# Latent attention: one step for a pair of heads, scores in two row tiles, causal mask added by TensorE

## The chip, the cores and the metric

The kernel runs on one core of a Trainium2 chip. The metric is device time in microseconds (us), from the start to the end of one execution; lower is better. Engines are named as in the profile: PE is TensorE's matmul, PEld its weight load, DVE is VectorE, ACT is ScalarE, POOL is GpSimd, SP is the queue that issues most DMAs. PSUM is the accumulator memory of PE: 8 banks of 512 float32 in each of 128 partitions.

## What is computed

A sandwich of two transformer layers on x of 1024 x 256. Each of the four parts is `x = x + layernorm(part(layernorm(x)))`: a 16-head attention without mask over one sequence of 1024, a ternary feed-forward part, a latent attention, and a feed-forward part whose weights are looked up in a table of 16 values. The change is in the third part, the latent attention, reduced here to what matters (1024 positions, 16 heads, latent width 64):

```python
c_kv = x @ Wdkv.T                                  # 1024 x 64, shared by all heads
q_lat = einsum('bhtd,hdl->bhtl', q, k_eff)         # a 64-wide query for each head
scores = einsum('bhtl,bsl->bhts', q_lat, c_kv) / sqrt(16)
scores = where(causal, scores, finfo.min)          # 16 heads x 1024 x 1024, lower triangle
attn = softmax(scores)                             # float32
ctx = einsum('bhts,bsl->bhtl', attn, c_kv)
y = einsum('bhtl,hld->bhtd', ctx, v_eff)           # 16 wide for each head
```

## The kernel before

Everything stays on the chip between the parts. Each engine has its own list of steps in program order (`order_of_latent` for this part), and semaphores tie the lists together. A step such as `("row_max", h, i8, part)` is read by all engines: each issues what is its own.

Heads are taken in pairs p (heads 2p and 2p+1) and in four groups g of two pairs. For a pair, these steps follow one another:

- `project` (line 1238 on PE): query and key rows of the pair into one PSUM bank. ACT writes a first part (line 1515, for keys also line 1520), then DVE (line 1802, queries) or POOL (line 2021, keys; line 1811 on DVE for the pair 0) subtracts. The keys of the two heads stand in different halves of the 128 partitions of `KT[p % 4]`, with zeros in the other half (`keys_zero` on POOL), so that one product over 128 partitions with a query that holds both heads gives one head's scores.
- `row_max` (line 1250 on PE, line 1829 on DVE): for each head and each block i8 of 128 queries the scores against the keys up to the diagonal, in one or two parts of at most 512 columns. DVE adds the mask, writes the sum back into PSUM and takes the row maximum in one custom instruction, which a short register read follows.
- `shift` (line 1260 on PE, line 1839 on DVE): the maxima of half of the positions are transposed by PE and subtracted from the queries by DVE, so that the exponent later needs no bias.
- `weights` (line 1271 on PE, line 1529 on ACT, line 2028 on POOL): scores again, transposed (keys on partitions), for one head and one block k of 128 keys; ACT takes the exponential into the buffer `ET`, POOL clears what lies above the diagonal in the first 128 columns. In the last group they are called `weights3` (lines 1296, 1539 and 2035) and are taken by halves of the positions.
- `combine` (line 1285 on PE; `combine3`, line 1310): four heads of a group at once, each in a column tile of 32 of PE's 128 columns, accumulated into banks 6 and 7.
- `heads_out` (line 1320): the result is transposed and divided by its sum.

PSUM banks 0 to 5 are a ring. Every product except `combine` takes the next bank in program order, and PE may write it once the engine that read that bank six takes earlier has released it:

```python
def take_ring(step, release):
    i = take(step, "ring", 6)
    BANK[step] = (i, free_ring[i])
    free_ring[i] = release
```

What stands next to what is set by `merge`, which interleaves two lists of steps in proportion to written costs: `behind(g)` holds the weights, shifts and combines of group g, `ahead(g)` the maxima and projections of the next pairs. In each group five combines (k from 0 to 4) stand among many weights; then the maxima of the group's next pair stand almost alone, with four projections between them; then come the three last combines, and the next group's weights start.

## Time and profile before

| | before |
|---|---|
| runs | 936.48 us median of 3 (935.08 to 939.54) |
| profiled execution, own time | 935.9 us |
| its span in the profile | 934.2 us |
| mean granted PE clock | 0.98 of full speed |
| latent attention, scores and combines | about 676 to 872 us of the span |

The span is what the trace covers; about 1.7 us of the profiled execution lie around it. The stage of the change is about a fifth of the span. "Idle before" is the time for which an engine stood still ahead of an instruction, with what ended it; a matmul's end is modelled, so the distance between two starts tells more than a matmul's duration.

### The profile page before, as it was taken

The numbers are of one execution on the slowest core, as the hardware profiler recorded it, in microseconds if no ns is written. First come the engines' busy times: TensorE is split into PE (matmuls) and PEld (weight loads), VectorE is DVE, ScalarE is ACT, GpSimd is POOL, SyncE is SP. The second block draws the span as 40 slices with busy tenths as digits, with TensorE's granted clock in tenths as the row PEclk, the third lists the DMA queues.
The fourth block names the chain that finished last, engine by engine and source line by source line (L and its number), as shares of the span: only waits on it lengthen the run. The fifth ranks groups of instructions, "written<-read, shape, count | busy, mean of one in ns | idle before, by whom it ended". The sixth has DMA issues, their size and how long they took to land.

```text
span 934.2 us, 12935 instructions
## 1 busy us (share of the span) xinstructions
PE 845.1 (90%) x4314; PEld 584.5 (63%) x4314; DVE 763.8 (82%) x1567; ACT 590.6 (63%) x990; POOL 413.8 (44%) x425
## 2 busy tenths in 40 slices
PE   4799989999999999999999998688877999998996
PEld 2566666676577577667667665457654555554686
DVE  3588999899998999999999998575599787876635
ACT  3476866776777666667667667364555767657533
POOL 2124444444344357778777771161323434433301
PEclk9999999999999999999999999789989999999999
DMA  3379757868777678668768767130000000000001
GB/s 110 65 154 170 138 111 167 175 129 149 167 154 147 128 136 158 136 128 158 155 109 147 130 133 144 35 105 1 1 1 0 1 1 1 2 1 1 1 1 45
DMA packets 276851, 86.29 MB, mean 92 GB/s; under 512 B 267568, under 2 KB 272432, under 8 KB 276400
## 3 DMA queue, kind: packets, MB, share of 16 engines
q1 hardware_dynamic: 275504, 80.05, 44.0%
q0 software_dynamic: 992, 5.34, 2.0%
q8 instruction: 34, 0.56, 0.3%
q14 instruction: 33, 0.27, 0.1%
q10 hardware_dynamic: 288, 0.07, 0.1%
HBM read 17.29 MB, written 1.05 MB: 20 GB/s over the span
## 4 chain that ended last, share of the span: by engine, by line
PE 51%; DVE 28%; issue 8%; ACT 7%; DMA 4%; POOL 1%; SPq 0%; ACTq 0%; POOLq 0%; DVEq 0%
PE ps L1033 11%; PE ps L1034 10%; PE ps L1035 10%; DVE nmax L1644 6%; DVE EP L1659 5%; PE ps L1056 4%; DVE ps L1829 3%; PE ps L1070 3%; PE ps L1285 3%; PE ps L1271 3%; DMA ET<-EP 2%; DVE ptm L1743 2%; PE ps L1250 2%; ACT EP L1435 1%; DVE st L1574 1%
## 5 line engine op out<-in xcount | busy, mean ns | idle before, releaser
L1435 ACT ACTIVATE EP<-ps,rinv 128x1024 f16<-128x1024 f32 x128 | 142.7, 1115 | 52.8 <-DVE rinv L1654 51.6
L1659 DVE SCALAR_TENSOR_TENSOR EP<-ps,rinv,EP 128x1024 f16<-128x1024 f32 x128 | 163.7, 1279 | 11.1 <-ACT EP L1435 10.4
L1425 ACT ACTIVATE ps<-ps,nmax 128x1024 f32<-128x1024 f32 x128 | 139.5, 1090 | 36.7 <-DVE nmax L1644 36.0
L1644 DVE TENSOR_REDUCE nmax<-ps 128x1 f32<-128x1024 f32 x128 | 154.9, 1210 | 1.4 <-PE ps L1035 1.2
L1966 POOL TENSOR_TENSOR wgu<-wgu,ptm 128x688 f32<-128x688 f32 x60 | 100.7, 1679 | 42.8 <-DVE ptm L1743 40.2
L1033 PE MATMUL ps<-ET,VH 128*128 128x512 f16 x256 | 98.8, 386 | 21.0 <-DMA ET<-EP 15.1
L1033 PE MATMUL ps<-KH,QH 128*128 128x512 f32 x256 | 106.6, 416 | 8.4 <-DVE KL L1626 4.7
L1966 POOL TENSOR_TENSOR wdn<-wdn,ptm 128x512 f32<-128x512 f32 x45 | 58.6, 1303 | 95.4 <-DVE ptm L1743 93.9
L1035 PE MATMUL ps<-KH,QL 128*128 128x512 f32 x256 | 100.6, 393 | 0.0
L1034 PE MATMUL ps<-KL,QH 128*128 128x512 f32 x256 | 100.3, 392 | 0.0
L1034 PE MATMUL ps<-ET,VH 128*128 128x512 f16 x256 | 98.2, 384 | 0.0
L1035 PE MATMUL ps<-ET,VL 128*128 128x512 f16 x256 | 98.0, 383 | 0.0
L1529 ACT ACTIVATE ET<-ps 128x512 f32<-128x512 f32 (+3 forms) x144 | 62.5, 498 | 36.9 <-PE ps L1271 36.2
L1829 DVE CUSTOM_DVE_ANT_0 ps<-ps,tern 128x512 f32<-128x512 f32 (+3 forms) x128 | 71.7, 603 | 15.0 <-PE ps L1250 14.9
L1893 POOL TENSOR_TENSOR rs<-ve,mhalf 128x4 f32<-128x4 f32 (+1 forms) x21 | 19.4, 922 | 123.1 <-DVE ve L1579 98.4
L1033 PEld LDWEIGHTS ps<-ET,VH 128*128 128x128 f16 x256 | 25.2, 98 | 61.0 <-DMA ET<-EP 21.1
L1033 PEld LDWEIGHTS ps<-KH,QH 128*128 128x128 f32 x256 | 48.2, 188 | 23.8 <-issue 6.8
L2028 POOL TENSOR_SCALAR_AFFINE_SELECT ET<-ET 128x128 f32<-128x128 f32 x96 | 28.2, 294 | 64.1 <-ACT ET L1529 57.3
L1033 PE MATMUL ps<-XH,wqh 128*128 128x512 f32 x128 | 55.0, 430 | 1.5 <-DVE VL L1636 1.0
L1035 PEld LDWEIGHTS ps<-KH,QL 128*128 128x128 f32 x256 | 48.0, 188 | 11.0
L1034 PEld LDWEIGHTS ps<-KL,QH 128*128 128x128 f32 x256 | 48.3, 189 | 7.8
L1034 PE MATMUL ps<-XL,wqh 128*128 128x512 f32 x128 | 51.7, 404 | 0.0
(237 smaller groups left out, 2166.7 us busy)
## 6 DMA issues: line engine op xcount, KB each, us to landing
wqr<-in_wqk SPq DMA_DIRECT2D x16, 256.0 KB, 3.8
wgu<-in_tern POOLq DMA_DIRECT2D x3, 1024.0 KB, 6.4
wvr<-in_wv SPq DMA_DIRECT2D x8, 256.0 KB, 4.3
wor<-in_wo SPq DMA_DIRECT2D x16, 128.0 KB, 3.1
ET<-EP SPq DMA_TRANSPOSE x128, 4.4
X<-in_x SPq DMA_DIRECT2D x2, 512.0 KB, 6.1
prw<-in_down_idx POOLq DMA_DIRECT2D x2, 256.0 KB, 6.2
tern<-in_l_wuq_rep SPq DMA_DIRECT2D x1, 512.0 KB, 4.6
```

The source lines that it names most:

```text
L1033: e.matmul(dst, lh, rh, start=first, stop=False)
L1034: e.matmul(dst, lh, rl, start=False, stop=False)
L1035: return e.matmul(dst, ll, rh, start=False, stop=last)
L1056: mm = e.matmul(ps[:, 2 * r + o, :], l, m, start=i == 0, stop=i == len(pairs) - 1)
L1425: e.activation(bank, bank, ACT.Exp, bias=nmax[:, c:c + 1], scale=1.0, accum_out=rsum[:, c:c + 1]).then_inc(exped.sem, 1)
L1435: e.mul(EP[:, n % NE_RING, 0, :], SB(u, j), rinv[:, c:c + 1]).then_inc(e_hi.sem, 1)
L1529: e.activation(ET[:, r, c:c + n1], ps[:, BANK[(*step, c)][0], n - n1:n], ACT.Exp).then_inc(weight_exped.sem, 1)
L1644: e.tensor_reduce(nmax[:, c:c + 1], SB(u, j), AX.X, ALU.max, negate=True).then_inc(maxed.sem, 1)
L1659: e.scalar_tensor_tensor(out=EP[:, n % NE_RING, 1, :], in0=SB(u, j), scalar=rinv[:, c:c + 1], in1=EP[:, n % NE_RING, 0, :], op0=ALU.mult, ...
L1829: e.tensor_tensor_reduce(src, src, mask[:, m0:m0 + n], 1.0, -3.0e38 if part == 0 else half, ALU.add, ALU.max, NM[:, p % 2, i8, col:col + 1 ...
L1966: e.tensor_tensor(dst, dst, ptm[:, v % 2, 0:n], ALU.add).then_inc(lut_added.sem, 1)
L2028: e.affine_select(out=tile, in_=tile, compare_op=ALU.is_ge, fill=0.0, base=0, pattern=[[1, P]], channel_multiplier=-1).then_inc(masked.sem, 1)
```

## The change

Scores, maxima, exponentials and selections are now steps of a pair, not of a head.

1. Keys: each pair has its own 128 x 1024 tile, one head in partitions 0 to 63 and the other in 64 to 127. The zero halves, and the POOL memsets that wrote them, are gone. A pair's key subtraction is one instruction over 128 partitions, not two over 64.
2. Scores: for each step PE issues two products of 64 rows each, one in each row tile (`tile_position` (0, 0) and (64, 0)), into two neighbouring banks.
3. Mask: for the part that holds the diagonal, PE adds the mask with two more products (a 128 x 128 identity by a 128 x 128 mask, both bfloat16, over the full 128 rows).
4. Maxima: DVE takes them with one ordinary reduction over both banks; for blocks of two parts a short `join_max` takes the larger. Nothing is written back into PSUM.
5. Exponentials and selections: one ACT instruction and one POOL instruction for both heads.
6. The ring: scores of a pair take two banks, starting at an even one, so six banks are three pairs. A product that needs one bank and stands between two pairs leaves the bank beside it unused.

```diff
 def maxima(p):
-    return [(0.1 + 0.001 * cuts(P * (i8 + 1))[part][1], ("row_max", 2 * p + hh, i8, part))
-            for i8 in range(8) for part in range(1 + i8 // 4) for hh in range(2)]
+    return [(0.1 + 0.002 * cuts(P * (i8 + 1))[part][1], ("row_max", p, i8, part))
+            for i8 in range(8) for part in range(1 + i8 // 4)] + [(0.05, ("join_max", p))]
...
-    KT = [QH, QL, KH, KL]
+    KT = [t[:, i, :] for t in (KL, QH, QL, KH) for i in range(2)]
+    halves = [slice(0, 64), slice(64, 128)]
...
+    def take_ring_pair(step, release):
+        count["ring"] += count["ring"] % 2
+        i = take(step, "ring", 6)
+        count["ring"] += 1
+        BANK[step] = (i, free_ring[i:i + 2])
+        free_ring[i] = free_ring[i + 1] = release
...
@@ PE, row_max @@
-    e.matmul(ps[:, i, 0:n], QT(p)[:, i8 * P:i8 * P + P], KT[p % 4][:, hh, c:c + n],
-             start=True, stop=True).then_inc(max_scored.sem, 1)
+    for hh, rows in enumerate(halves):
+        mm = e.matmul(ps[:, i + hh, 0:n], QT(p)[rows, i8 * P:i8 * P + P], KT[p][rows, c:c + n],
+                      start=True, stop=part < i8 // 4, tile_position=(64 * hh, 0))
+    if part == i8 // 4:
+        w.wait_ge(*mask_set["ident"])
+        for hh in range(2):
+            mm = e.matmul(ps[:, i + hh, P * i8 - c:P * i8 - c + P], ident_b, mask_b,
+                          start=False, stop=True)
+    mm.then_inc(max_scored.sem, 1)
...
@@ PE, weights (weights3 alike) @@
-    e.matmul(ps[:, i, 0:n], KT[p % 4][:, h % 2, k * P:k * P + P], Q2[p % 4][:, q0:q0 + n],
-             start=True, stop=True).then_inc(weighed.sem, 1)
+    for hh, rows in enumerate(halves):
+        mm = e.matmul(ps[:, i + hh, 0:n], KT[p][rows, k * P:k * P + P], Q2[p % 4][rows, q0:q0 + n],
+                      start=True, stop=True, tile_position=(64 * hh, 0))
+    mm.then_inc(weighed.sem, 1)
...
@@ DVE, row_max @@
-    e.tensor_tensor_reduce(src, src, mask[:, m0:m0 + n], 1.0, -3.0e38 if part == 0 else half,
-                           ALU.add, ALU.max,
-                           NM[:, p % 2, i8, col:col + 1] if last else half).then_inc(row_maxed.sem, 1)
+    e.tensor_reduce(NMC[p % 2][:, i8, :] if i8 < 4 else m1[:, p % 2, i8 - 4, part, :],
+                    ps[:, i:i + 2, 0:n], AX.X, ALU.max).then_inc(row_maxed.sem, 1)
...
@@ ACT, weights @@
-    e.activation(ET[:, r, c:c + n1], ps[:, BANK[(*step, c)][0], n - n1:n],
-                 ACT.Exp).then_inc(weight_exped.sem, 1)
+    e.activation(ET[:, 2 * r:2 * r + 2, c:c + n1], ps[:, i:i + 2, n - n1:n],
+                 ACT.Exp).then_inc(weight_exped.sem, 1)
```

Where one group ends and the next begins, PE's program holds these rows before (the opening of group 2: the two short combines, line 1285, then weights of line 1271, maxima of line 1250, shifts of line 1260; the number behind x counts equal rows in a run):

```order
L1285 MATMUL ps<-ET,VX 32x256 x4
L1285 MATMUL ps<-ET,VX 32x128 x4
L1271 MATMUL ps<-XL,QH 128x512 x2
L1250 MATMUL ps<-KH,XH 128x256 x4
L1271 MATMUL ps<-XL,QH 128x512 x2
L1250 MATMUL ps<-KH,XH 128x384 x2
L1250 MATMUL ps<-KH,XH 128x512
L1271 MATMUL ps<-XL,QH 128x512
L1271 MATMUL ps<-XL,QH 128x384
L1250 MATMUL ps<-KH,XH 128x512
L1250 MATMUL ps<-KH,XH 128x384
L1260 MATMUL ps<-ident,NM 128x128 x4
```

At the same place PE's program holds these rows after (line 1284 weights, line 1256 maxima, line 1261 masks, line 1273 shifts, line 1299 combines; each x2 of lines 1284 and 1256 is one pair, one product in each row tile):

```order
L1299 MATMUL ps<-ET,VX 32x256 x4
L1299 MATMUL ps<-ET,VX 32x128 x4
L1284 MATMUL ps<-XL,QL 128x512 x4
L1256 MATMUL ps<-KH,XH 128x256 x2
L1261 MATMUL ps<-tern 128x128 x2
L1256 MATMUL ps<-KH,XH 128x256 x2
L1261 MATMUL ps<-tern 128x128 x2
L1256 MATMUL ps<-KH,XH 128x384 x2
L1261 MATMUL ps<-tern 128x128 x2
L1256 MATMUL ps<-KH,XH 128x512 x2
L1261 MATMUL ps<-tern 128x128 x2
L1273 MATMUL ps<-ident,NM 128x128 x4
```

Both heads' weights now stand together (two pairs of 512 columns in a row), then four pairs of maxima, each with its masks, where weights and maxima of single heads took turns; the first shift stands behind the fourth pair of maxima.

DVE's program at the same place before: a custom instruction for each head, a register read behind each, one shift (line 1839) between them.

```order
L1829 ISA ps,NM<-ps,tern 128x384
L1829 ISA NM 128x1
L1829 ISA ps,NM<-ps,tern 128x512
L1829 ISA NM 128x1
L1829 ISA ps,NM<-ps,tern 128x512
L1829 ISA NM 128x1
L1839 TENSOR_TENSOR Q<-XH,ps 128x512
L1829 ISA ps,M<-ps,tern 128x384
```

And after: line 1846 is the join of the pair before, line 1839 now the reductions, line 1854 the shifts, line 1819 and line 1862 a projection's subtraction and a `heads_out`.

```order
L1846 TENSOR_TENSOR NM<-M 128x8
L1839 TENSOR_REDUCE NM<-ps 128x2 x4
L1854 TENSOR_TENSOR XL<-XH,ps 128x512
L1839 TENSOR_REDUCE M<-ps 128x2
L1854 TENSOR_TENSOR XL<-XH,ps 128x512
L1839 TENSOR_REDUCE M<-ps 128x2 x2
L1819 SCALAR_TENSOR_TENSOR XH<-ps,pat,R 128x512
```

A reduction of both heads stands where two custom instructions and two reads stood; the order of maxima, shifts and projections is kept.

## Rows read from the trace of the kernel before

**Rows 1.** Busy time by stretch: us, each engine's busy (instructions), granted clock, DMA.

```profile
676.00:727.00 51.00, 40.99 (x157) 26.51 (x155) 46.00 (x149) 29.43 (x55) 14.44 (x21) 0.91 0.00 1
...
727.00:747.00 20.00, 19.35 (x134) 10.82 (x134) 13.16 (x44) 13.90 (x31) 10.11 (x21) 1.00 0.01 1
747.00:773.00 26.00, 23.71 (x108) 13.97 (x106) 22.24 (x76) 17.07 (x35) 11.25 (x19) 1.00 0.01 1
...
839.00:872.00 33.00, 29.38 (x178) 13.72 (x172) 19.35 (x58) 25.03 (x61) 14.37 (x42) 1.00 0.01 2
```

**Rows 2.** Chain that ended last, by line: 676 to 727, then 727 to 840 us.

```profile
by line: DVE ps L1829 37.1%; issue 18.4%; ACT R L1515 6.9%; DVE NM L1829 5.7%; PE ps L1271 4.3%; DVE XL L1839 3.5%; DVE Q L1802 3.0%; DVE M L1829 2.8%; ACT tern L1520 2.8%; DVE QH L1811 2.7%; ACT ET L1529 2.3%; DVE XL L1591 2.1%; DVE XH L18
...
by line: PE ps L1285 24.4%; PE ps L1271 21.1%; PE ps L1250 16.0%; DVE ps L1829 9.9%; issue 7.9%; ACT ET L1529 4.2%; ACT R L1515 3.5%; PE ps L1238 3.0%; PE ps L1260 2.9%; PE ps L1320 1.7%; DVE XH L1802 1.3%; DVE NM L1829 1.3%; ACT tern L1520
```

**Rows 3.** Pieces of that chain, 773 to 798 us: start, us, what.

```profile
773.23 1.85 PE ps L1285 x16
...
777.75 1.64 PE ps L1285 x16
...
780.06 0.23 PE ps L1271
780.29 0.23 PE ps L1250
...
782.46 1.43 PE ps L1285 x16
...
789.12 0.99 PE ps L1285 x8
...
797.47 0.78 PE ps L1285 x8
```

**Rows 4.** DVE maxima and a plain reduction, groups: busy, mean ns | idle.

```profile
L1644 DVE TENSOR_REDUCE nmax<-ps 128x1 f32<-128x1024 f32 x128 | 154.9, 1210 | 1.4 <-PE ps L1035 1.2
...
L1829 DVE CUSTOM_DVE_ANT_0 ps<-ps,tern 128x512 f32<-128x512 f32 x64 | 44.5, 720 | 6.1 <-PE ps L1250 6.0
L1829 DVE CUSTOM_DVE_ANT_0 ps<-ps,tern 128x128 f32<-128x128 f32 x16 | 4.6, 313 | 6.1 <-PE ps L1250 6.1
```

**Rows 5.** DVE busy of line 1829 alone: opening stretch, and all stretches.

```profile
676.00:727.00 51.00, 32.54 (x123) 0.91 0.00 1
...
sum 163.00, DVE 106.09; mean DVE 17.68
```

**Rows 6.** Exponentials on ACT, groups.

```profile
L1425 ACT ACTIVATE ps<-ps,nmax 128x1024 f32<-128x1024 f32 x128 | 139.5, 1090 | 36.7 <-DVE nmax L1644 36.0
...
L1529 ACT ACTIVATE ET<-ps 128x512 f32<-128x512 f32 x60 | 34.2, 605 | 17.5 <-PE ps L1271 17.2
```

**Rows 7.** Timeline: a product whose bank was late, and its reader.

```profile
753.36 0.39 PE L1271 MATMUL ps<-XL,QL 128*128 128x256 f32 x1 [0.16 <-DVE M L1829]
...
753.84 0.38 ACT L1529 ACTIVATE ET<-ps 128x256 f32<-128x256 f32 x1 [0.43 <-PE ps L1271]
```

**Rows 8.** Timeline of PE, opening of group 2.

```profile
801.06 0.73 PE L1271 MATMUL ps<-XL,QH 128*128 128x512 f32 x2
...
805.75 0.60 PE L1260 MATMUL ps<-ident,NM 128*128 128x128 f32 x4
806.10 0.91 PE L1250 MATMUL ps<-KH,XH 128*128 128x256 f32 x2
807.05 0.98 PE L1271 MATMUL ps<-XL,QH 128*128 128x512 f32 x2
807.99 0.74 PE L1238 MATMUL ps<-CS,QW 128*128 128x512 f32 x2
...
817.44 1.06 PE L1285 MATMUL ps<-ET,VX 128*32 128x512 f32 x8
```

**Rows 9.** A weight load of the scores, and the key split of pair 0.

```profile
L1250 PEld LDWEIGHTS ps<-KL,XH 128*128 128x128 f32 x48 | 8.9, 188 | 3.4 <-DVE XH L1802 1.2 <-DVE NM L1829 0.7 <-DVE M L1829 0.5
...
L1811 DVE TENSOR_TENSOR QH<-tern,R 64x512 fp32r<-64x512 f32 x4 | 2.7, 687 | 1.9 <-ACT tern L1520 1.8
```

## Prediction before the run

> **What bounds the kernel now.** I first read the busy time by stretch [rows 1], because the stage of the change (about 676 to 872 us) has no single bound. From 676 to 727 us DVE is busy for 46.0 of 51 us: the maxima of the first two pairs. From 727 to 747 us, where combines stand among weights, PE is busy for 19.4 of 20 us; two more such stretches follow (773 to 791 and 817 to 839), 60 us in all. Between them lie stretches like 747 to 773 us: PE 23.7, DVE 22.2 and ACT 17.1 of 26 us, so nothing is free and nothing is full. In the last group (839 to 872 us) ACT is busy for 25.0 of 33 us.
>
> The chain says the same [rows 2]. In the opening stretch DVE's maxima (line 1829) hold 37% of it. From 727 to 840 us PE holds it: the combines 24.4%, the scores of lines 1271 and 1250 together 37.1%, which is 42 us; DVE's maxima hold 9.9%. The pieces [rows 3] show how it runs there: score after score at 0.23 us for 512 columns, then a combine, with no wait between them.
>
> So PE work removed would show in 60 us, DVE work in some 100 us. That is the most the change can move; what it can lose is in the ring of banks.
>
> **PE.** Before, 336 score products with a mean of 453 columns (counted in the program): at 0.23 us for 512 columns [rows 3], 68 us. If the two row tiles run together, half goes: -34 us of PE time. The trace has no row tile. Its nearest rows are the combines in four column tiles [rows 3]: 1.85, 1.64 and 1.43 us for 1024, 896 and 768 columns, so 0.21 us for every 128 columns, all four heads and both passes of float32 together. Their single instructions, laid end to end, would need several times that, so tiles do run at once in this kernel. 1024 columns at that rate are 1.70 us, and 0.15 us is left for entering and leaving the tiles. New are 64 steps with two mask products. A 128-column product lies between 0.06 us (a quarter of 0.23) and 0.09 us (four transposes in 0.35 us, [rows 8]), and each mask step also leaves the row tiles and comes back, 0.15 us: about 0.3 us a step, 19 us. In program order the mode changes rise from 64 to 227; apart from the 128 around masks that is 35 more, 3 us at half of 0.15. PE's balance is -12 us if row tiles overlap, and +22 us if not.
>
> [...]
>
> **DVE.** Line 1829 is busy for 106.1 us over eight pairs [rows 5], 13.3 us a pair, each of its 192 instructions with a register read. Its forms give 1.06 ns a column (720 against 313 ns over 384 columns, [rows 4]). The plain reduction of line 1644 takes 1210 ns for 1024 columns [rows 4], so 125 ns beside its columns. A pair needs 12 reductions over 9216 columns: 9.8 + 1.5 = 11.3 us, and a join, at most 0.2 us. That saves 1.9 us a pair; if reductions can't overlap at their ends as the custom ones do, about 1.2 us. Over the stage it is 9 to 15 us. Pair 0's key split, four instructions of 0.69 us [rows 9], becomes two: -1.4 us.
>
> **ACT and POOL.** A pair of 512 columns costs 1.09 us at most (line 1425, [rows 6]) against twice 0.605 us; back to back the two overlap, so I give ACT nothing. POOL halves its key splits and loses its memsets, but nothing of this lies in the chain [rows 2]; I count 0, and if it showed, at most one 0.7 us piece.
>
> **The ring.** This is where I think the gain goes. Six banks were six tiles; now they are three pairs, and a projection, shift or heads_out between two pairs takes a pair's place. In program order the ring's takes rise from 456 banks to 495, 39 of them unused. A place is held from the first write until its reader is done. From a late bank's product to its reader's start it is 0.48 us [rows 7]; where the weights are there earlier I take 0.42, with masks 0.62, and 0.05 us back to PE. Reading takes 1.06 us (exponentials of 1024 columns), 1.21 us (maxima of 1024).
>
> I placed the rows of the opening of group 2 under these rules, from the end of the last combine. Two exponentials' scores fill places 1 and 2 at 0 and 0.25, the first maxima place 3 at 0.5. The second maxima need place 1: the exponential runs from 0.42 to 1.48, so 1.53. The third need place 2: the second exponential ends at 2.44, so 2.5. The fourth follow at 2.95 and the first shift at 3.4 in the places that DVE has left. The next maxima wait for the third reduction (4.0), so 4.05; the second shift waits for the fourth (5.15), so 5.2. Two more places on, the next weights start at 6.8, the projection of queries at 8.4, and the next group's first combine at 18.3. In the trace [rows 8], counted from 801.06 us, the second shift stands at 4.7, the weights at 6.0, the projection at 6.9 and the combine at 16.4. The same rules with six single places put that combine at 16.5, so they can be trusted to a few tenths. **This opening gets 1.9 us longer**; it occurs twice in full (758 to 773 and 801 to 817 us).
>
> The same placement from 775.08 (end of a combine) to 801.06 us puts the next combines at 2.5, 7.0 and 14.15 us, and the first short one at 23.6; in the trace they stand at 2.7, 7.4, 14.0 and 22.4 us [rows 3]. The end comes at 26.1 against 26.0 us. PE no longer works there all the time, but waits for places as long: **no gain in the combine stretches**.
>
> A late place costs more with two loads: a score's load is 188 ns [rows 9], and the second tile's may follow the first. Between 0 and 0.2 us for each of some 186 places, three at a time, is 0 to 12 us; most waits overlap others, so I take +3, a quarter.
>
> **Sum.** Opening stretch: 32.5 us of maxima [rows 5] are 2.45 pairs, -4.7 at best, -2.9 at 1.2 us a pair, and -1.4 for the key split; part returns as waits for places, so -4 (bounds -6 and 0). Combine and maxima stretches 0. Two openings +3.8. Late places +3. Last group: half its scores come free, but ACT sets the pace, -1. Together +1.8: 935.9 + 1.8 = 937.7 us for the profiled execution, which stands 0.6 us under the median of the runs. I predict **938.3 us**.
>
> **Rivals.**
> - *Places turn over in time.* If a pair's fill hides behind the other two, the engines' own savings count: opening -4, maxima stretches -5 (37 us of maxima are 2.8 pairs at 1.9), combine stretches -6 (143 score products there, half of some 26 us, less 22 mask steps at 0.3), last group -2: 17 us less, 919 us. For it: in [rows 1] ACT and DVE have 6 to 7 of 20 us idle in a combine stretch. Against it: the placement above, which holds for the trace before.
> - *Row tiles follow one another.* Place: every pair of products. PE keeps its 68 us and adds masks: in the combine stretches, already full, 22 mask steps are +7 us; every place is held 0.2 us longer, 186 places by three, +12; with -4, +3.8 and -1 it ends 17 us later, 954 us. It decides from the point at which a second product of 512 columns starts over 0.15 us after the first. For it: no row here shows a row tile of float32r. Against it: the column tiles of [rows 3].
> - *PE slows down.* Thinner PE work could bring the lower granted clock: the mean was 0.91 in the opening stretch, where PE was busy for 41 of 51 us, and 1.00 afterwards [rows 1]. If 727 to 872 us ran at 0.91, PE's part of that chain, about 100 us, grows by 10: 947 us.
>
> [...]
>
> **How the numbers follow.** Forecast 0.50, with an own range of 930 to 947 (opening and late places at either bound); places in time 0.27; row tiles in turn 0.14; clock 0.09. A difference under 0.5% (931.8 to 941.2 us) is about what a measurement of this kernel can't tell from no change. Of the forecast 0.04 falls below it, 0.28 inside, 0.18 above; of the first rival 0.26 below and 0.01 inside; the other two, but for 0.01 inside, above. That makes faster 0.30, same 0.30, slower 0.40. The range is 918 to 955: from just under the first rival's 919 to just over the second's 954.
>
> **What would show it.** Right: the second product of a pair starts at once after the first; reductions of 1024 columns take about 1.2 us; in the combine stretches PE has waits for ACT and DVE that it did not have; an opening from a group's last combine to the next group's first takes 18 us, not 16.4; the first combine of group 0 (727.1 us before) comes about 4 us earlier. Wrong: combines as close as 1.4 us to each other's ends with idle DVE would mean that places were never short; a pair's products 0.23 us apart, or a granted clock of 0.5 among the scores, would mean one of the slower rivals.

## The result, and the profile after

The changed kernel takes 962.37 us (median of 4 runs, 960.60 to 962.94) against 936.13 us (4 runs) for the kernel before beside it: a ratio of 1.0271, 95% interval 1.0241 to 1.0300. The profiled execution took 960.6 us, its span is 958.9 us (934.2 before) and its mean granted clock 0.955 (0.980 before). The forecast was 938.3 us, its range 918 to 955 us: the time lies outside.

The place comes first. The starts and ends of combines (line 1285 before, 1299 after) cut the stage into stretches that can be compared one by one:

| stretch, us | before | after | forecast | measured |
|---|---|---|---|---|
| to the first combine of group 0 | to 727.1 | to 734.1 | -4 | +7.0 |
| combines of group 0 | 31.1 | 35.2 | 0 | +4.1 |
| opening of group 1 | 15.0 | 18.6 | +1.9 | +3.6 |
| combines of group 1 | 27.8 | 31.3 | 0 | +3.5 |
| opening of group 2 | 16.4 | 20.0 | +1.9 | +3.6 |
| combines of group 2 | 22.5 | 26.2 | 0 | +3.7 |
| from there to the next stage's first product | 32.6 | 31.8 | -1 | -0.8 |

That is 24.7 us, the whole difference of the spans. (The forecast had 3 us more for late places, without a stretch of their own.) Nothing is lost outside the stage, and within it every stretch but the last loses. The stage's first projection comes even 1.6 us earlier (670.3 us, before 671.9), so from there to the first combine the loss is 8.6 us.

The page's slices of the whole span (tenths of the granted clock in 40 equal slices) show what else changed:

```profile
PEclk9999999999999999999999998999786979899999
```

The stage begins with the 29th digit. Before, the 30th digit was an 8, and all the others of the stage were 9. Cut into stretches of 20 us, the changed kernel reads as follows (us, then for each engine busy us and instructions, granted clock, DMA share, GB/s; these answer to [rows 1]):

```profile
660.00:680.00 20.00, 13.44 (x84) 10.59 (x83) 10.94 (x37) 10.62 (x19) 4.54 (x9) 0.97 0.00 0
680.00:700.00 20.00, 17.36 (x72) 10.31 (x72) 14.01 (x18) 7.54 (x14) 1.74 (x2) 0.77 0.01 1
700.00:720.00 20.00, 17.57 (x72) 8.93 (x71) 14.24 (x17) 10.89 (x16) 2.46 (x4) 0.74 0.00 0
720.00:740.00 20.00, 18.85 (x78) 8.06 (x76) 10.91 (x15) 8.64 (x12) 3.80 (x6) 0.58 0.00 1
740.00:760.00 20.00, 18.32 (x126) 7.92 (x124) 10.93 (x16) 10.38 (x15) 4.52 (x9) 0.91 0.00 1
760.00:780.00 20.00, 16.02 (x101) 7.57 (x99) 15.95 (x21) 9.10 (x13) 4.17 (x6) 0.95 0.00 1
780.00:800.00 20.00, 17.32 (x100) 7.39 (x102) 8.06 (x10) 13.28 (x19) 5.38 (x9) 0.80 0.01 2
800.00:820.00 20.00, 17.55 (x130) 7.81 (x122) 13.69 (x18) 9.99 (x16) 5.40 (x9) 1.00 0.00 1
820.00:840.00 20.00, 15.80 (x74) 7.57 (x78) 13.24 (x17) 11.95 (x16) 3.31 (x6) 0.81 0.00 0
840.00:860.00 20.00, 17.69 (x138) 7.57 (x130) 10.99 (x16) 9.02 (x14) 4.12 (x8) 0.93 0.00 1
860.00:880.00 20.00, 17.16 (x124) 6.87 (x125) 11.04 (x20) 11.44 (x18) 7.00 (x16) 0.91 0.00 1
```

The last number but two of a row is the clock. It falls and rises through the whole stage; a stretch at 0.58 is a mean of parts at 0.50 and at 1.00 (0.50 from 710.0 to 736.9 us, 1.00 from 737.1 to 747.0 us), and no profile of this case has a third level. It is no sign of a PE without work: from 700 to 710 us, just ahead of the longest low part, PE was busy for 8.2 of 10 us, and the kernel before for 7.6 us there at a clock that stayed at 1.00. What PE lost to the clock can be read off as an estimate: busy time times what the clock lacks to 1.00. Over these rows that is 28.6 us (18.85 x 0.42 = 7.9 us in the worst). The kernel before lost 4.2 us in the same way, all of it before 700 us (15.22 and 17.26 us busy at 0.87). The 24.4 us between them are PE work, and turn into time only where PE sets the end.

The chain's combines show the same; these pieces (start, us, what) answer to [rows 3]:

```profile
787.96 3.57 PE ps L1299 x16
794.44 1.64 PE ps L1299 x16
799.32 1.43 PE ps L1299 x16
...
807.13 1.00 PE ps L1299 x8
816.69 0.78 PE ps L1299 x8
...
839.25 3.57 PE ps L1299 x16
```

The first combine of groups 1 and 2 takes 3.57 us, where [rows 3] have 1.85. From 794 to 819 us the clock was full, and combines cost what they did before. Yet from the second combine of group 1 to its first short one it is 22.25 us (794.44 to 816.69), against 19.72 us before (777.75 to 797.47): the low clock isn't all of it.

The other engines did what was forecast. Groups by form of VectorE's maxima and ScalarE's exponentials (busy, mean ns | idle before, releaser), to be read beside [rows 4, 6]:

```profile
L1839 DVE TENSOR_REDUCE M<-ps 128x2 f32<-128x1024 f32 x32 | 38.9, 1221 | 19.0 <-PE ps L1261 11.8 <-PE ps L1256 7.1
...
L1545 ACT ACTIVATE ET<-ps 128x1024 f32<-128x1024 f32 x30 | 30.1, 1025 | 27.5 <-PE ps L1284 27.4
```

1221 ns stands against 1.21 us in the working, 1025 ns against 1.06 us. VectorE's maxima fell from 106.1 us [rows 5] to 90.1 us (two groups, 64.0 and 26.1), and the stage got no shorter by it: what stands behind the bar is idle time, 19.0 and 27.5 us, spent on waiting for PE's products.

Last, the row tiles. PE's timeline (start, us, what [idle before]) with the clock at 1.00:

```profile
819.14 0.73 PE L1284 MATMUL ps<-XL,QL 64*128 64x512 f32 x4
819.71 0.28 PE L1256 MATMUL ps<-KH,XH 64*128 64x256 f32 x2
...
822.36 0.51 PE L1256 MATMUL ps<-KH,XH 64*128 64x512 f32 x2
822.80 0.28 PE L1261 MATMUL ps<-tern 128*128 128x128 bf16 x2
822.92 0.61 PE L1273 MATMUL ps<-ident,NM 128*128 128x128 f32 x4
```

Four products of 512 columns take 0.57 us with a change of tiling mode on one side (819.14 to 819.71), two take 0.44 us with a change on either side (822.36 to 822.80), and two mask products 0.12 us. Taking off 0.10 us for each side (worked out below), a pair of 512 columns costs 0.24 us, what one product over 128 rows cost [rows 3]. The tiles do run at once: of the stage's 192 pairs 187 have less than 10 ns between the starts of their two products, the others at most 59 ns.

For the column tiles the trace of before shows it too. A product of the combines leaves two records, 16 for the 8 products of 512 columns, and a record of 512 columns lasts 596 ns in the mean (144 of line 1285). End to end 16 of them would take 9.5 us, and even at 0.23 us each, a score product's distance from start to start, 3.7 us; they take 1.85.

### The profile page after: what moved, and what is told of

Read it like the earlier page. It is cut to its first block, busy times and chain, and to the rows that moved or that the text cites. A ratio compares the mean times of both kernels' runs of the same rounds, so it can differ in the third digit from the quotient of the medians.

```text
span 958.9 us, 12544 instructions
## 1 busy us (share of the span) xinstructions
PE 853.3 (89%) x4442; PEld 567.2 (59%) x4442; DVE 750.7 (78%) x1285; ACT 583.0 (61%) x894; POOL 376.9 (39%) x341
## 3 DMA queue, kind: packets, MB, share of 16 engines
q1 hardware_dynamic: 275504, 79.59, 42.9%
## 4 chain that ended last, share of the span: by engine, by line
PE 52%; DVE 27%; ACT 9%; issue 7%; DMA 3%; POOL 1%; SPq 0%; ACTq 0%; POOLq 0%; DVEq 0%
PE ps L1039 10%; PE ps L1040 10%; PE ps L1041 10%; DVE nmax L1661 5%; DVE EP L1676 5%; PE ps L1062 4%; PE ps L1299 3%; PE ps L1076 3%; PE ps L1256 3%; DVE M L1839 2%; DVE ptm L1760 2%; DMA ET<-EP 2%; ACT ET L1545 2%; PE ps L1244 1%; ACT EP L1450 1%
## 5 line engine op out<-in xcount | busy, mean ns | idle before, releaser
L1839 DVE TENSOR_REDUCE M<-ps 128x2 f32<-128x1024 f32 (+1 forms) x64 | 64.0, 1020 | 35.2 <-PE ps L1261 26.0
L1545 ACT ACTIVATE ET<-ps 128x1024 f32<-128x1024 f32 (+2 forms) x72 | 55.5, 811 | 58.6 <-PE ps L1284 58.4
L1039 PEld LDWEIGHTS ps<-ET,VH 128*128 128x128 f16 x256 | 25.1, 98 | 60.9 <-DMA ET<-EP 21.1
L2026 POOL TENSOR_SCALAR_AFFINE_SELECT ET<-ET 128x256 f32<-128x256 f32 x48 | 19.6, 409 | 103.5 <-ACT ET L1545 102.6
```

Source lines behind the costliest of these rows:

```text
L1039: e.matmul(dst, lh, rh, start=first, stop=False)
L1545: e.activation(ET[:, 2 * r:2 * r + 2, c:c + n1], ps[:, i:i + 2, n - n1:n], ACT.Exp).then_inc(weight_exped.sem, 1)
L1839: e.tensor_reduce(NMC[p % 2][:, i8, :] if i8 < 4 else m1[:, p % 2, i8 - 4, part, :], ps[:, i:i + 2, 0:n], AX.X, ALU.max).then_inc(row_maxe ...
```

## Experiments

Three theories. **Clock**: products over 64 rows bring TensorE's lower clock. **Places**: three double places in the ring hold PE up more than six single ones. **Masks and modes**: the 128 mask products, and 163 more changes of tiling mode, are what PE has too much of. A tiling mode is what the profile writes before a product's shape: 128*128 for the whole array, 64*128 in row tiles, 128*32 in column tiles. Every ratio is to the kernel before, run beside it; differences in us between kernels are differences of such ratios at 935 us.

### The clock, the places and the masks apart

`e1_half_rows`: the kernel before, where a score product takes its head's rows alone (the other two products of scores likewise).

```diff
-e.matmul(ps[:, i, 0:n], QT(p)[:, ...], KT[p % 4][:, hh, c:c + n], start=True, stop=True)
+rows = slice(64 * hh, 64 * hh + 64)
+e.matmul(ps[:, i, 0:n], QT(p)[rows, ...], KT[p % 4][rows, hh, c:c + n],
+         start=True, stop=True, tile_position=(64 * hh, 0))
```

> The kernel before (one head, one bank, one step at a time; masks by GpSimd and VectorE as before), but each score product takes only the 64 rows that its head's keys fill, in the row tile of those rows, where it took 128 rows of which 64 were zero. Same values, same number of products and steps. [...] Theory 2 (three double places in the ring in place of six single ones) and theory 3 (the mask products on PE): neither is in this kernel, so 934 to 939 us. Where neighbouring steps of the two heads overlap in their row tiles, PE saves some us: down to 930.

948.41 us, ratio 1.0151 (1.0118 to 1.0184), mean clock 0.957. The clock theory had 946 to 961 us here, with a clock of 0.50 in parts of the stage. Two stretches ahead of the first combine, first of the kernel before, then of this one:

```profile
700.00:710.00 10.00, 7.58 (x33) 4.47 (x31) 8.00 (x24) 5.67 (x11) 0.29 (x1) 1.00 0.00 0
710.00:722.00 12.00, 9.82 (x40) 6.02 (x40) 11.92 (x44) 5.91 (x13) 6.30 (x8) 1.00 0.00 1
```

```profile
700.00:710.00 10.00, 8.24 (x30) 4.17 (x30) 8.04 (x27) 4.17 (x8) 0.27 (x1) 0.91 0.00 0
710.00:722.00 12.00, 11.80 (x31) 6.19 (x31) 9.21 (x31) 7.05 (x13) 4.12 (x6) 0.50 0.00 0
```

Up to 710 us both kernels do the same steps in the same order, and PE is about as busy in one as in the other. Then the clock falls in the second alone, to 0.50 for the whole of the next stretch, where PE fills 11.80 of 12 us with fewer instructions than before. The rows of the products differ, and with them the tiling mode: the stage has 164 changes of mode, before 64. Changes alone don't lower the clock (`g4_mode_changes` below: 125 more, mean clock 0.979). So 64-row products bring the lower clock, in a kernel without pairs, doubled places or masks.

The time is lost where the clock is low. From the stage's first projection to the first combine e1 loses 7.8 us, and in the combines of group 0 2.2 us. From there to the end of group 1's combines (768.0 to 811.0 us, clock 1.00 but for the last 4 us) it takes 43.1 us, before 42.9, although 96 products over 64 rows and 26 more changes of mode stand there.

From 700 to 710 us PE was no less busy in the kernel whose clock fell (8.24 against 7.58 us), so its busy time alone does not tell which level it gets.

`e2_full_rows`: the kernel after, without row tiles. `e3_no_mask`: the kernel after, without the mask products. `e4_full_no_mask`: both.

```diff
 # e2, e4 (all three places of scores)
-mm = e.matmul(ps[:, i + hh, 0:n], QT(p)[rows, ...], KT[p][rows, c:c + n], ..., tile_position=(64 * hh, 0))
+mm = e.matmul(ps[:, i + hh, 0:n], QT(p)[:, ...], KT[p][:, c:c + n], ...)
 # e3, e4
-mm = e.matmul(ps[:, i + hh, P * i8 - c:P * i8 - c + P], ident_b, mask_b, start=False, stop=True)
```

> The kernel after, but every score product over all 128 rows and without a row tile; the scores of each head become the sum of both heads', so the values change and the work of all other engines doesn't. PE loses the overlap of the two products (a pair of 512 columns 0.45 us in place of 0.28 us, over the stage about 20 to 30 us of PE's busy time). Theory 1 (clock): granted clock over the stage back at 0.98 or more, no combine of 512 columns over 2 us outside the first rise of the clock, and the time falls to 935 to 948 us although PE has more to do. Theories 2 and 3: the time stays at 960 us or rises, to 985 at most.

> The kernel after without the 128 mask products on PE; the maxima are then taken over the unmasked diagonal block, so the shift of a row can be larger. Theory 3 (mask products and their mode changes): 128 products of about 0.1 to 0.25 us on PE gone, time 945 to 952 us. Theory 1: the mask products are the only ones among the scores that use all 128 rows, so without them the clock is no better or falls further: 957 to 972 us. Theory 2: 956 to 962 us.

> The two edits before together: score products over all 128 rows (each head's scores are the sum of both heads'), and no mask products. What is left of the change is the pairs, the ring of three double places, the plain reductions and the exponentials over both heads. Theory 1: granted clock 0.98 or more, 930 to 942 us. Theory 2: each opening of a group 2 to 4 us longer than before, with DVE and ACT waiting less elsewhere, 938 to 948 us even at full clock. If neither the clock nor the mask is the cause: 960 us or more.

In e2 and e4, and in the kernels built on e4, each head's scores are the sum of both heads'; the work of the other engines is the same.

- e2: 955.36 us, ratio 1.0235 (1.0194 to 1.0276). The clock is back (1.00 from 700 to 860 us), but not the time. The clock theory, which had it at 935 to 948 us, can't be the whole.
- e3: 960.56 us, ratio 1.0294 (1.0234 to 1.0354), clock 0.927 to 0.942, after 0.943 to 0.955: with the only 128-row products among the scores gone the clock falls further, and nothing is won. Its four runs, with no edit between them, are the longer the lower their mean clock: 957.4, 958.4, 962.7 and 968.7 us at 0.942, 0.940, 0.936 and 0.927.
- e4: 951.33 us, ratio 1.0182 (1.0138 to 1.0226), clock 0.986. At full clock, with nothing of row tiles or masks left, 17 us stay. This is the surprise of the first four runs.

### What stays at full clock: order, operations or places

Three kernels on the base of e4. `e5_full_weights_single` gives the exponentials' products a place and an operation for each head, `e6_full_maxima_single` the maxima's, `e7_full_all_single` both; the steps keep the order of the kernel after.

```diff
 # e6, e7 (e5 and e7 likewise for the exponentials)
-take_ring_pair(step, row_maxed.mark(*at))
+for hh in range(2):
+    take_ring((*step, hh), row_maxed.mark(*at, hh))
 ...
-e.tensor_reduce(NMC[p % 2][:, i8, :] ..., ps[:, i:i + 2, 0:n], AX.X, ALU.max)
+e.tensor_reduce(out, ps[:, i, 0:n], AX.X, ALU.max)  # for each head
```

> The last kernel (full rows, no masks on PE; 951.3 us, granted clock 0.986), but the score products for the exponentials take one single place for each head and ScalarE takes one exponential for each head, in the same order of steps; the maxima stay pairs. Left out as there: each head's scores are the sum of both heads', and no mask before the maxima. Theory 2 (what is left at full clock is the three double places of the ring): a good half of the 16 us comes back, 938 to 945 us, if the pairs of the exponentials are what PE waits for; about 950 us if only the pairs of the maxima matter. Rival, the order of the steps (two heads in one step, so the merge of the lists falls otherwise): no change, 949 to 953 us.

> The same base, but the maxima take one single place and one VectorE reduction for each head, and the exponentials stay pairs. Same parts left out. Theory 2: the other part of the 16 us, 938 to 946 us; the opening of a group (the end of one group's last combine to the next group's first) gets 1 to 2 us shorter, as the next pair of heads' maxima stand between. Rival, the order: 949 to 953 us.

> The two edits together: every score product in a single place with an operation of its own, six in flight, in the order of steps of the kernel after. Same parts left out. Theory 2: 931 to 938 us, the kernel before's time, or a little less since VectorE's reductions have no mask to add. Rival, the order of the steps: 947 us or more, since the order is the changed kernel's. In between says that both count.

e5 951.22 us (ratio 1.0186, 1.0151 to 1.0220), e6 948.53 us (1.0142, 1.0107 to 1.0177), e7 937.99 us (1.0044, 1.0028 to 1.0060). One kind alone gives back nothing or 4 us, both give back 12.9 us. The order of the steps, together with the cheaper maxima, leaves 4 us (e7); what the order costs by itself isn't shown. And singles have both more places and shorter operations. Two kernels change the places alone: `h1_five_places` and `h2_four_places` are e7 with a smaller ring.

```diff
-i = take(step, "ring", 6)
+i = take(step, "ring", 5)   # h2: 4
```

> The kernel with single places, full rows and no masks (938.0 us with six places; the parts left out as there), with a ring of five places. Theory 2, places: PE waits more, 940 to 945 us. Rival (it was the double operations of VectorE and ScalarE that cost 13 us in pairs, as each holds its engine twice as long, and not the number of places): 937 to 940 us.

> The same with four places. Theory 2: three double places, which single steps between pairs often hold alone, are worth four to five single ones, so this comes near the 951.3 us of the pairs: 946 to 960 us. Rival, the double operations: under 942 us.

h1 948.99 us (1.0156, 1.0134 to 1.0177), h2 965.57 us (1.0326, 1.0297 to 1.0354), both at a mean clock of 0.973 or more. With the operations unchanged, the sixth place is worth 10.5 us and the fifth 15.9 us. Three double places (e4, 1.0182) come out like five single ones, within the intervals. So places alone can cost what the pairs cost; whether the longer operations have a share in the 12.9 us no run here shows.

Is the loss due to the places that a single step between two pairs leaves unused? `h3_any_pair` (on e4) and `h4_after_any_pair` (on the kernel after) let a pair start at any place but the last.

```diff
-count["ring"] += count["ring"] % 2
+count["ring"] += count["ring"] % 6 == 5
```

> The kernel with pairs, full rows and no masks (951.3 us; the parts left out as there), where a pair may start at any place but the last, so that a single step between two pairs leaves no place unused: 39 unused places over the stage become fewer than half. Theory 2 with the unused places as its cause: 942 to 948 us. If it is the three pairs themselves, not the places lost to single steps: 949 to 953 us.

> The kernel after with that same edit of the ring, and nothing else; same values. With single places the row tiles were 3.8 us under the kernel after, so this can give 0 to 4 us: 958 to 962 us. If the unused places were what costs beside the low clock: 955 us or less.

h3 960.32 us (1.0278, 1.0256 to 1.0301), h4 968.23 us (1.0369, 1.0320 to 1.0419): 9 us worse on either base, where I had expected a gain or nothing. A pair that lies across two earlier pairs has to wait for both their readers; that explanation is argued, not tested. Using the unused places in this way gains nothing.

### Row tiles with six single places, and a lifted clock

`g1_rows_single` is the kernel after (row tiles, masks on PE) with single places and operations as in e7. `g2_fill` is the kernel after with two products over 128 rows ahead of each pair of maxima of the first two pairs of heads, into the same places; `g3_rows_single_fill` is g1 with one such product a step.

```diff
 # g2, ahead of the pair's products
+if p < 2:
+    for hh in range(2):
+        e.matmul(ps[:, i + hh, 0:n], QT(p)[:, ...], KT[p][:, c:c + n], start=True, stop=True)
```

> The kernel after with its row tiles and its masks on PE, but single places: one place, one VectorE reduction or one ScalarE exponential for each head, in the order of steps of the kernel after. Same values. Theory 2 (doubled places): the 13 us that single places gave back at full clock come back here too, 946 to 952 us; what stays over the kernel before is then the clock and the mode changes. Theory 1 alone: 957 to 965 us, as the row tiles and so the clock are as after. If the mode changes of PE (0.10 us each by the rows, some 160 more than before) were all of the rest, the granted clock would have to be as before, which I don't expect.

> The kernel after, with additional work on PE and nothing taken away: ahead of each pair of products of the maxima of the first two pairs of heads, two products over all 128 rows into the same places, which the pair then overwrites. Same values; 48 products, some 8 us of PE at full clock, and 48 mode changes at most. Theory 1: the granted clock of 680 to 740 us (0.77, 0.74, 0.58 after) rises to 0.9 or more, and the first combine, at 734.1 us after, comes 3 to 8 us earlier although PE does more; 952 to 959 us. Against it: more work makes it 965 us or more.

> Single places and row tiles, with one product over all 128 rows ahead of each step of the maxima of the first two pairs of heads, overwritten as above. Same values. Theories 1 and 2 together: 938 to 947 us, 4 to 8 us under the same kernel without the additional products, the first combine at 722 to 728 us; it could come under the kernel before only if the overlap of the row tiles pays for the mode changes in the combine stretches.

g1 958.54 us (1.0268, 1.0231 to 1.0304): single places give nothing back here, against my 946 to 952 us. The stretch from 820 to 840 us, first of e7, then of g1:

```profile
820.00:840.00 20.00, 19.50 (x135) 10.98 (x127) 13.87 (x30) 10.79 (x26) 4.56 (x9) 1.00 0.00 1
```

```profile
820.00:840.00 20.00, 19.50 (x71) 9.35 (x70) 10.96 (x21) 11.38 (x22) 4.17 (x6) 0.59 0.00 0
```

With six places PE is full in both, in g1 at 0.59. (The counts don't compare: e7 is already at the combines of group 2 there, which are many short products, while g1 is mostly in the opening ahead of them.) Row tiles and masks together cost 20.9 us over e7.

g2 962.30 us (1.0300, 1.0274 to 1.0326), g3 961.35 us (1.0285, 1.0244 to 1.0326): both miss what I expected. The products that do nothing did lift the clock for a while; the row of g2 answers to the one above from 700 to 720 us, at 0.74:

```profile
700.00:720.00 20.00, 18.00 (x91) 10.07 (x89) 13.29 (x16) 9.94 (x15) 2.10 (x3) 1.00 0.00 1
```

But the next 20 us have 0.74 again, and the first combine came at 735.7 us, no earlier than 734.1. That 128-row work lifts the clock is borne out there; that it pays is not. That the products cost PE what the clock gave is argued.

### What a change of mode costs

`e8_half_rows_weights`: e1 with 64 rows for the products of the exponentials alone, and 128 for those of the maxima.

```diff
 # e1, products of the maxima
-e.matmul(ps[:, i, 0:n], QT(p)[rows, ...], KT[p % 4][rows, hh, c:c + n], ..., tile_position=(64 * hh, 0))
+e.matmul(ps[:, i, 0:n], QT(p)[:, ...], KT[p % 4][:, hh, c:c + n], start=True, stop=True)
```

> The kernel before, with the 64-row products in row tiles for the exponentials alone; the products of the maxima stay over 128 rows. Same values. The question is the dose: in the kernel with both kinds over 64 rows (948.4 us) the granted clock was 0.74, 0.71 and 0.53 between 680 and 740 us, where nearly only products of maxima and projections run, and 1.00 from 740 to 800, where the exponentials' products run among the combines. If the clock follows the share of 64-row products in a stretch, this kernel keeps 1.00 nearly throughout and takes 930 to 937 us (gain only where two neighbouring products overlap); if any 64-row product pulls the clock down, 940 to 948 us.

960.02 us (1.0292, 1.0224 to 1.0360), 14 us worse than with all products over 64 rows: both ways of the dose miss. The clock stayed at 1.00 from 700 to 740 us, although products over 64 rows run there from 705 us on, and fell to 0.69 and 0.74 at 760 to 780 and 820 to 840 us. And something else had come in. PE's timeline of this kernel, at full clock:

```profile
749.66 0.38 PE L1272 MATMUL ps<-XL,QH 64*128 64x256 f32 x1
749.97 0.44 PE L1250 MATMUL ps<-KL,XH 128*128 128x384 f32 x1
750.35 0.38 PE L1272 MATMUL ps<-XL,QH 64*128 64x256 f32 x1
750.66 0.44 PE L1250 MATMUL ps<-KL,XH 128*128 128x384 f32 x1
```

From start to start it is 0.31 us for 256 columns and 0.38 for 384, where 64 and 128 rows take turns. Between products of one mode it is 0.12 and 0.18 us (medians of the kernel before). Each of these distances holds exactly one change, so a change costs 0.19 to 0.20 us. The same with 512 columns: 0.23 alone, 0.34 with a change on one side and 0.43 with one on either side. A change stands between two products and lengthens both, by 0.10 us each. Beside the short mask products less shows: in g1 a pair of 256 columns, its two masks and the way back to the next pair take 0.53 us, where a pair alone takes 0.12, and with 512 columns it is 0.64 against 0.23. That is 0.41 us a mask step, and with 0.12 us for the two masks 0.15 for each of its two changes. **A change of mode costs 0.15 to 0.20 us.**

In program order over the stage (660 to 900 us) the timelines have 64 changes before, 227 after, 164 in e1 and 228 in e8, so e8 spends some 33 us of PE more on changes (an estimate: 164 x 0.20). Its combines of group 1 (782.6 to 814.7 us) show it at a clock of 1.00 throughout: 46 changes and 32.1 us, before 14 and 28.0. In e1, where the clock is full, added changes cost nothing that shows (above); neighbouring products of the two heads run at once there (one starts at 779.14 us, the next at 779.15), which may pay for them, but no run tests that apart.

`g4_mode_changes` buys changes alone: e7 with a product of 16 columns in a row tile ahead of each first part of the maxima.

```diff
+if part == 0 and hh == 0:
+    e.matmul(ps[:, i, 0:16], ident_b[0:64, :], mask_b[0:64, 0:16], start=True, stop=True, tile_position=(0, 0))
```

> The kernel with single places, full rows and no masks (938.0 us, granted clock 0.979; the parts left out as there), with a product of 16 columns in a tile of 64 rows ahead of each first part of the maxima, overwritten by the score behind it: 64 products, 128 mode changes more, hardly any columns. At 0.10 us for a change, as the rows read, and 0.02 us for the product PE has some 14 us more; where PE sets the end all of it shows: 944 to 952 us at a granted clock of 0.97 or more. If a change costs 0.2 us, 955 us or more; if it hides, 937 to 940 us.

944.82 us (1.0115, 1.0094 to 1.0135), clock 0.979: 6.6 us over e7 for 125 changes more, 0.053 us each. From start to start each added product takes 0.11 us and lengthens its two neighbours by 0.10 us each, some 20 us of PE for 64 of them (an estimate). A third of it shows; the rest hides in PE's waits.

### Is the kernel before short of places itself?

`k1_half_places` lets two products of 256 columns share a place in the kernel before; `k2_half_places_last_rows` does so up to the last group and takes row tiles there.

```diff
+if n == 256 and key in HALF:           # second head: the other half of the place
+    i, at = HALF.pop(key)
+    BANK[step], OFF[step] = (i, None), 256
 ...
-w.wait_ge(*max_scored[h, i8, part])
+w.wait_ge(*max_scored[h + (hh == 0 and cuts(wide)[part][1] == 256), i8, part])
```

> The kernel before, with one edit of its ring: two products of 256 columns for the two heads of a pair (maxima, exponentials, last group) share one place, 256 columns each, and its first reader waits until both are written. Full rows, single operations, same values. If places are what the kernel before runs short of (five cost 11.0 us, four 27.6 us against six), a third of the score products now hold half a place, some 0.8 place more on average: 2 to 6 us under the kernel before, 928 to 933 us. If the sixth place was the last that counted: 933 to 936 us; if the later start of the first reader outweighs it: 937 us or more.

> The same, but in the last group (the stretch from 839 to 872 us before) the products take a whole place each and only their head's 64 rows, in its row tile. No maxima stand there, and each of these products has combines or transposes on both sides as before, so that mode changes hardly rise. Same values. Against the kernel with half places: 0 to 3 us less if neighbouring heads overlap and the clock holds; 3 us or more above it if the clock falls there too.

k1 942.62 us (1.0080, 1.0056 to 1.0103), k2 941.02 us (1.0067, 1.0049 to 1.0086). Both are slower than before. That the first reader's wait for its neighbour outweighs the free halves is the likely reason, but not shown apart. Whether a seventh place of a full bank would help stays open, since that wasn't tried. Row tiles in the last group gain nothing that the intervals can tell.

## Why the prediction was wrong

**Right in kind.** The second product of a pair starts with the first (under 10 ns behind it in 187 of 192 pairs). Reductions took 1.22 us, exponentials 1.03. The last group was put at -1 us and measured -0.8; but e7, without row tiles, has -0.5 there, so this is no sign of the overlap.

**Failed: the clock.** The sum's -4 us for the first opening counts VectorE's savings alone; its 0 for the combine stretches and +1.9 for a later opening come from rows at full clock [rows 3, 8]. None of these terms has a price for a lower clock, which was left to a rival of 10 us (0.91 from 727 to 872 us) with a chance of 0.09. The granted clock fell to 0.50 for parts of nearly every stretch, and by the estimate above cost PE 24.4 us more than before. e1 shows it without pairs, double places or masks. The forecast said what would show it, a granted clock of 0.5 among the scores, but drew its price from [rows 1], where PE worked on 128 rows throughout; such rows can't price products over 64.

**Failed: the ring.** "No gain in the combine stretches" was entered as 0, and an opening as 1.9 us. The combine stretches lost 3.5 to 4.1 us each and the openings 3.6. Part of that is the clock's, but at full clock, without masks and row tiles, e4 already loses 5.0 us from the stage's first projection to the first combine, 1.8, 2.8 and 3.3 us in the combine stretches and 2.7 us in each opening. e7, with single places, has 1.0, then -0.9, 0.9 and 1.0, then 1.9 and 0.7. Pairs alone cost 12.9 us (e7 to e4), where the sum had 6.8 us for two openings and late places. The placement by hand was near: from the second combine of group 1 to the first short one it gave 21.1 us, and at full clock 22.25 were measured, where the kernel before had 19.72. The error was to call such a stretch neutral because its end came out within 0.1 us.

**Mis-sized: PE's balance.** It was put at -12 us at full clock: -34 for the overlap, +19 for masks, +3 for other changes. A mask step was put at 0.3 us and measured 0.41, another change at 0.075 and measured 0.20, so the balance is -34 + 64 x 0.41 + 35 x 0.20 = -1 us (an estimate): by it PE had nothing to win even at full clock. The 0.15 us around a combine, from which the price was read, leaves out the products on either side of it, which take 0.10 us longer each in the kernel before. The sum had no term for this balance, so the forecast was not off by it.

**Right, but worth nothing.** VectorE's savings came (16 us of maxima), and the first combine still came 7.0 us later, not 4 earlier. In the changed opening PE's scores and VectorE's maxima wait for each other, at a clock of 0.50 from 710 to 734 us.

Put together as two ways from before to after, at 935 us:

| step | us | step | us |
|---|---|---|---|
| order, plain reductions, merged POOL work (e7) | +4.1 | the same (e7) | +4.1 |
| pairs in double places (e4) | +12.9 | row tiles and masks, single places (g1) | +20.9 |
| masks on PE (e2) | +5.0 | pairs in double places (after) | +0.3 |
| row tiles (after) | +3.4 | | |

The two costs don't add. With row tiles PE runs at the low clock and is full anyway (the row of g1), so a place is free by the time PE gets to it; that is argued from that row, since no run here had row tiles at full clock throughout. PE's account of the row tiles leaves room for that: from e7 to g1 -34 + 26 + 7 + 29 (35.4 us lost to the clock against 6.3) gives +28 us of PE, of which 20.9 show. The steps for masks on PE and for row tiles, 5.0 and 3.4 us, lie within the intervals of their ratios; e7's 4.1 us is clear of them. Open is why the clock falls where it does: e8, with fewer 64-row products than e1, kept it at 1.00 from 720 to 740 us, where e1 had 0.53, and lost it at 760 to 780 us, where e1 had 1.00. Open too is what the order of the steps and the longer operations cost by themselves.

## What to carry to other kernels

A product cut to half the rows in order to run two at once must be priced at the lower clock too (0.50 for 12 us in e1): look at the granted clock of a kernel that does the cut alone before counting the overlap. Where readers release places of a ring, count places and not bytes: merging two operations into one that holds two places was a loss here (12.9 us from e7 to e4), and five places against six already cost 10.5 us. Count changes of tiling mode in program order (0.15 to 0.20 us each here) before letting steps of different modes take turns, and read the price of a change from the products on both sides of it.

## What was not expected of the hardware

In e1 the granted clock stood at 0.50 for 12 us while PE's instructions filled 11.80 of them, and before it fell PE was no less busy than the kernel before, where it stayed at 1.00; products over 64 rows in place of 128 set the two apart. Products that do nothing, over 128 rows, brought it back to 1.00 from 700 to 720 us (g2; 0.74 without them). A change of tiling mode lengthens the product ahead of it as well as the one behind it (512 columns: 0.23 us alone, 0.34 with a change on one side, 0.43 with one on either). And with score products of both 64 and 128 rows the kernel (e8, 960.0 us) was slower than with either alone (948.4 and 935 us).
